# Cross-attention with a top-ten pick: the key-bias term moved to VectorE, and the second query projection placed behind the second weighted sum

## The reference

```python
scores = jnp.einsum('bnd,d->bn', base_hidden, score_w[0]) + score_b[0]
_, topk_idx = jax.lax.top_k(scores, TOPK)                       # TOPK = 10
sparse_hidden = jnp.take_along_axis(base_hidden, topk_idx[:, :, None], axis=1)
q = (sparse_hidden @ Wq.T + bq).reshape(B, TOPK, H, dh).transpose(0, 2, 1, 3)
k = (scaffold_hidden @ Wk.T + bk).reshape(B, -1, H, dh).transpose(0, 2, 1, 3)
v = (scaffold_hidden @ Wv.T + bv).reshape(B, -1, H, dh).transpose(0, 2, 1, 3)
logits = jnp.einsum('bhqd,bhkd->bhqk', q, k) * scale
attn = jax.nn.softmax(logits, axis=-1)
o = jnp.einsum('bhqk,bhkd->bhqd', attn, v).transpose(0, 2, 1, 3).reshape(B, TOPK, D)
attn_out = o @ out_w.T + out_b
return base_hidden.at[jnp.arange(B)[:, None], topk_idx].set(attn_out)
```

## Time and profile before

| | us |
|---|---|
| median of 3 runs | 140.95 (140.5 to 141.01) |
| the profiled execution | 140.47 |
| its span in the profile | 138.7 |
| TensorE busy | 132.0 (95%), 1314 instructions |
| VectorE busy | 91.7 (66%), 252 instructions |
| ScalarE busy | 27.0 (19%) |
| DMA over the span | 270 GB/s mean |

### The profile page before, as it was taken

How to read it: one execution, slowest core, us unless ns; L and a number is a source line. 1 busy time by engine, 2 the same in 40 slices (tenths; PEclk the granted TensorE clock), 3 DMA queues, 4 the chain that set the end, 5 groups by cost and what they waited for, 6 DMA issues and landing times.

```text
span 138.7 us, 3144 instructions
## 1 busy us (share of the span) xinstructions
PE 132.0 (95%) x1314; PEld 125.6 (91%) x1314; DVE 91.7 (66%) x252; ACT 27.0 (19%) x59; POOL 10.9 (8%) x36
## 2 busy tenths in 40 slices
PE   6889999999998999999999999999999999999990
PEld 3168999999997899999999999999999999999970
DVE  4596697898993676487872565177228799875160
ACT  5132400070511250012140041004101400131120
POOL 7710000260030000000000000000000000000002
PEclk9999999999999999999999999999999999999999
DMA  3999999999614999799999897998795093000001
GB/s 68 405 427 416 409 405 405 414 443 428 268 40 129 425 426 419 291 343 316 395 379 294 319 438 224 318 409 308 240 285 217 5 322 131 0 0 5 0 5 50
DMA packets 7293, 37.52 MB, mean 270 GB/s; under 512 B 1040, under 2 KB 1040, under 8 KB 5104
## 3 DMA queue, kind: packets, MB, share of 16 engines
q1 hardware_dynamic: 6864, 37.00, 70.6%
q0 software_dynamic: 128, 0.33, 0.8%
q10 hardware_dynamic: 288, 0.01, 0.1%
HBM read 33.50 MB, written 3.83 MB: 269 GB/s over the span
## 4 chain that ended last, share of the span: by engine, by line
PE 63%; DVE 14%; DMA 13%; SPq 4%; issue 4%; POOLq 1%; POOL 0%; DVEq 0%
PE mix_ps L899 29%; PE logits_ps L862 24%; DMA x_sb<-x_lines_dram 11%; PE logits_ps L846 5%; DVE product L442 3%; DMA picked<-x_dram,row_idx 2%; DVE col_max L569 2%; SPq L220 2%; PE logits_ps L818 2%; DVE probs L603 1%; PE mix_ps L818 1%; SPq L209 1%; DVE q_diag L530 1%; POOLq L62 1%; PE logits_ps L784 1%
## 5 line engine op out<-in xcount | busy, mean ns | idle before, releaser
L899 PE MATMUL mix_ps<-probs,ctx_r 125*128 125x160 f32 x336 | 47.2, 300 | 0.0
L899 PEld LDWEIGHTS mix_ps<-probs,ctx_r 125*128 125x128 f32 x336 | 46.0, 190 | 0.3 <-issue 0.2
L862 PE MATMUL logits_ps<-qk,ctx_c 128*125 128x160 f32 x240 | 33.4, 299 | 0.0
L862 PEld LDWEIGHTS logits_ps<-qk,ctx_c 128*125 128x125 f32 x240 | 32.9, 188 | 0.0
L569 DVE TENSOR_REDUCE col_max<-logits_ps 125x160 f32<-125x480 f32 x16 | 10.1, 653 | 16.6 <-PE logits_ps L862 13.7
L846 PE MATMUL logits_ps<-qk,ctx_c 128*125 128x160 f32 x144 | 20.1, 300 | 0.0
L846 PEld LDWEIGHTS logits_ps<-qk,ctx_c 128*125 128x125 f32 x144 | 19.6, 188 | 0.1
L388 ACT ACTIVATE mix<-mix_ps 128x320 f32<-128x320 f32 x16 | 7.0, 440 | 62.7 <-PE mix_ps L899 57.7
L610 DVE TENSOR_REDUCE prob_sum<-probs 125x160 f32<-125x960 f32 x8 | 14.6, 1829 | 4.5 <-ACT probs L378 4.4
L378 ACT ACTIVATE probs<-probs 125x480 f32<-125x480 f32 x16 | 9.3, 602 | 25.3 <-DVE probs L603 25.3
L442 DVE CUSTOM_DVE_ANT_0 product<-x_sb,score_w_sb 112x513 f32<-112x513 f32 x14 | 10.0, 761 | 2.4 <-DMA x_sb<-x_lines_dram 2.4
(11 more groups left out here) (137 smaller groups left out, 100.0 us busy)
## 6 DMA issues: line engine op xcount, KB each, us to landing
ctx_r<-ctx_rows_dram SPq DMA_DIRECT2D x7, 1536.0 KB, 10.2
ctx_c<-ctx_cols_dram SPq DMA_DIRECT2D x6, 1500.0 KB, 8.9
x_sb<-x_lines_dram SPq DMA_DIRECT2D x8, 520.0 KB, 13.0
out_dram<-x_sb SPq DMA_DIRECT2D x8, 448.0 KB, 9.7
ctx_r<-ctx_rows_dram SPq DMA_DIRECT2D x3, 512.0 KB, 15.5
ctx_c<-ctx_cols_dram SPq DMA_DIRECT2D x2, 750.0 KB, 14.4
ctx_c<-ctx_cols_dram SPq DMA_DIRECT2D x4, 375.0 KB, 15.1
wq_sb<-wq_dram SPq DMA_DIRECT2D x1, 1024.0 KB, 8.0
```

The costliest lines, as they stand in the source:

```text
L862: last = nc.tensor.matmul(logits_ps[n][0:S_P, t // BANK_T, (t % BANK_T) * HQ:(t % BANK_T + 1) * HQ], ctx_c[n][:, f, t, :], qk[:, b, f, :], ...
L899: last = nc.tensor.matmul(mix_ps[half][:, f * HQ:(f + 1) * HQ], ctx_r[n][0:S_P, t, c:c + P], probs[n][:, t, :], start=(t == 0), stop=(t == ...
```

## The change

The key-bias term no longer passes TensorE. `key_heads`, `dot_key_bias` and `spread_key_dot` go, and with them GpSimd's clearing of `key_heads`. VectorE multiplies the masked queries by the key bias, `key_terms` (one instruction for the first group, four for the second), and `sum_key_terms` adds over the partitions: a transposing reduction over 128 partitions, three copies, a small reduction.

The second group's masked queries are made by one instruction a block (`spread_pairs`): it reads the projection in PSUM, adds the bias and multiplies by the mask, into `q_pairs`, whose order is head, batch, query. The fold waits block by block for them.

On TensorE the transposes stand ahead of the 22nd matmul of the second weighted sum and the projection behind its last.

```diff
-        q_diag = [sb(f"q_diag{g}", [P, DT, b1 - b0, HPT, TOPK])
-                  for g, (b0, b1) in enumerate(GROUPS)]
+        q_diag = [sb("q_diag0", [P, DT, FIRST, HPT, TOPK])]
+        q_pairs = sb("q_pairs", [P, DT, HPT, GROUPS[1][1] - GROUPS[1][0], TOPK])
...
-        key_rows = sb("key_rows", [QUAD, B, DT, HC])
+        key_terms = sb("key_terms", [P, B, DT, HPT, TOPK])
...
+            def spread_pairs():
+                b0, b1 = GROUPS[1]
+                nb = b1 - b0
+                for e in range(DT):
+                    dve.wait_ge(q_ps, 3 + e // 2)
+                    nc.vector.scalar_tensor_tensor(
+                        out=q_pairs[:, e, :, :, :].rearrange("p h b q -> p h (b q)"),
+                        in0=query_ps[1][e // 2][:, (e % 2) * nb * TOPK:(e % 2 + 1) * nb * TOPK]
+                        .unsqueeze(1).broadcast_to([P, HPT, nb * TOPK]),
+                        scalar=bias_sb[:, 0, e:e + 1],
+                        in1=head_mask[:, :].unsqueeze(2).broadcast_to([P, HPT, nb * TOPK]), op0=ALU.add, op1=ALU.mult)\
+                        .then_inc(pair_q_done, 1)
...
+            def first_key_terms():
+                dve.wait_ge(q_done, 2)
+                nc.vector.tensor_tensor(
+                    key_terms[:, 0:FIRST, :, :, :].rearrange("p b e h q -> p e b (h q)"),
+                    q_diag[0][:, :, :, :, :].rearrange("p e b h q -> p e b (h q)"),
+                    bias_sb[:, 1, :].unsqueeze(2).unsqueeze(3).broadcast_to([P, DT, FIRST, HC]), ALU.mult).then_inc(key_terms_done, DT)
+
+            def pair_key_terms():
+                dve.wait_ge(pair_q_done, DT)
+                for e in range(DT):
+                    nc.vector.tensor_scalar(key_terms[:, FIRST:B, e, :, :].rearrange("p b h q -> p h b q"), q_pairs[:, e, :, :, :],
+                                            bias_sb[:, 1, e:e + 1], None, ALU.mult).then_inc(key_terms_done, 1)
+
+            def sum_key_terms(g):
...
+                dve.wait_ge(key_terms_done, DT * (g + 1))
                 nc.vector.tensor_reduce(
-                    key_dot[:, b0:b1, :].rearrange("p b k -> p (b k)"),
-                    key_rows[:, b0:b1, :, :].rearrange("p b e c -> p (b e c)").rearrange("p (k c) -> p k c", c=QUAD),
-                    AX.X, ALU.add, apply_transpose=True).then_inc(key_dot_done, 1)
+                    quad_sum[:, 0, bs, :].rearrange("p b k -> p (b k)"),
+                    key_terms[:, bs, :, :, :].rearrange("p b e h q -> p (b e h q)").rearrange("p (k c) -> p k c", c=QUAD),
+                    AX.X, ALU.add, apply_transpose=True).then_inc(key_step, 1)
+                dve.wait_ge(key_step, at + 1)
+                for q in range(1, QUADS):
+                    nc.vector.tensor_copy(quad_sum[0:QUAD, q, bs, :], quad_sum[q * QUAD:(q + 1) * QUAD, 0, bs, :]).then_inc(key_step, 1)
+                dve.wait_ge(key_step, at + 4)
+                nc.vector.tensor_reduce(key_dot[:, bs, :], quad_sum[0:QUAD, :, bs, :].rearrange("p q b k -> p b k q"), AX.X, ALU.add)\
+                    .then_inc(key_dot_done, 1)
...
             def fold_pairs():
                 w = HPT // 2 * TOPK * (GROUPS[1][1] - GROUPS[1][0])
-                pe.wait_ge(q_done, 4)
                 pe.wait_ge(shifted, 2 * GROUPS[0][1])
...
                     for e in range(DT):
+                        if step == 0:
+                            pe.wait_ge(pair_q_done, e + 1)
                         for r in range(2):
                             rows = slice(r * P // 2, (r + 1) * P // 2)
                             last = nc.tensor.matmul(pair_ps[step % 2][r][:, e * w:(e + 1) * w],
                                                     wk_sb[rows, e, step * P:(step + 1) * P],
-                                                    q_diag[1][rows, e, :, 2 * r:2 * r + 2, :],
+                                                    q_pairs[rows, e, 2 * r:2 * r + 2, :, :].rearrange("p h b q -> p b h q"),
                                                     start=True, stop=True)
...
-            weigh(1, 1, {18: transpose_picked, 21: lambda: project_queries(1)})
+            weigh(1, 1, {21: transpose_picked})
+            project_queries(1)
             fold_pairs()
-            dot_key_bias(1)
```

More of the change, by code:

```diff
@@ L518, in move_idx, with spread_queries @@
                     nc.vector.tensor_copy(row_idx[k * QUAD:k * QUAD + m, :], idx_cols[0:m, k:k + 1]).then_inc(idx_ready, 1)
[L520 to L522 removed]
+            def spread_queries():
                 for half in range(2):
                     es = slice(2 * half, 2 * half + 2)
[L525 removed]
+                    dve.wait_ge(q_ps, half + 1)
                     nc.vector.tensor_tensor(
[L527 to L529 removed]
+                        q_sb[:, es, :, :], query_ps[0][half][:, 0:2 * FIRST * TOPK].rearrange("p (t b q) -> p t b q", t=2, b=FIRST),
+                        bias_sb[:, 0, es].unsqueeze(2).unsqueeze(3).broadcast_to([P, 2, FIRST, TOPK]), ALU.add).then_inc(q_biased, 1)
+                    dve.wait_ge(q_biased, half + 1)
@@ L530, in spread_queries @@
                     nc.vector.tensor_tensor(
-                        q_diag[g][:, es, :, :, :].rearrange("p t b h q -> p (t b) h q"),
-                        q_sb[g][:, es, :, :].rearrange("p t b q -> p (t b) q").unsqueeze(2).broadcast_to([P, 2 * nb, HPT, TOPK]),
-                        head_mask[:, :].unsqueeze(1).unsqueeze(3).broadcast_to([P, 2 * nb, HPT, TOPK]), ALU.mult)\
+                        q_diag[0][:, es, :, :, :].rearrange("p t b h q -> p (t b) h q"),
+                        q_sb[:, es, :, :].rearrange("p t b q -> p (t b) q").unsqueeze(2).broadcast_to([P, 2 * FIRST, HPT, TOPK]),
@@ L701, in _ @@
             sum_probs(1, 1)
-            spread_queries(1)
+            spread_pairs()
             copy_pairs()
-            spread_key_dot(1)
+            pair_key_terms()
+            sum_key_terms(1)
             for b in range(2, B):
@@ L819, in fold_pairs @@
                                                     wk_sb[rows, e, step * P:(step + 1) * P],
-                                                    q_diag[1][rows, e, :, 2 * r:2 * r + 2, :],
+                                                    q_pairs[rows, e, 2 * r:2 * r + 2, :, :].rearrange("p h b q -> p b h q"),
                                                     start=True, stop=True)
                     last.then_inc(pair_done, 1)
-            def dot_key_bias(g):
-                w = TOPK * (GROUPS[g][1] - GROUPS[g][0])
-                pe.wait_ge(key_heads_done, 1)
-                pe.wait_ge(q_biased, 2 * g + 2)
-                for e in range(DT):
-                    last = nc.tensor.matmul(key_ps[g][e * QUAD:(e + 1) * QUAD, 0:w], key_heads[:, e, :],
-                                            q_sb[g][:, e, :, :].rearrange("p b q -> p (b q)"), start=True, stop=True)
-                last.then_inc(key_dot_ps, 1)
             def logits_by_step(b, n, copied, between):
```

37 lines of the change are left out of this document (10 added, 27 removed).

## The result

| us | before | changed |
|---|---|---|
| median, 8 runs each | 140.43 (140.16 to 141.01) | 139.17 (139.04 to 139.86) |
| ratio, 95% interval | | 0.991 (0.9892 to 0.9927) |
| profiled execution | 140.47 | 139.44 |
| span | 138.7 | 137.7 |

The change makes the kernel 0.9% faster.

What follows compares the result with a forecast made beforehand. TensorE was taken to bound the kernel, waiting only 0.76 us for the gather and 0.31 us for `q_diag`. Gains of 0.79 + 0.24 = 1.03 us, taken from 140.95, gave 139.9 us, range 139.4 to 140.8.

Steps and rivals of the forecast that it cites:

- What bounds the kernel: TensorE, with two gaps between 41 and 47 us; time won by 51.09 is kept to the end.
- Step 1: Second weighted sum on TensorE: three matmuls move into the 0.76 us gather wait, projection goes last; 0.82 us.
- Step 2: First key-bias product leaves TensorE, 0.18 us, worth nothing alone; VectorE's added work hides before `x_sb`, about 1.1 us spare.
- Step 3: One masked VectorE instruction a block, 0.46 us each; the fold's step 0 ends at 47.06 instead of 47.85: 0.79 us.
- The signs named, two waits of 0.1 to 0.2 us: TensorE waits inside step 0 of the fold, expected in the profile if the forecast is right.
- The instruction at half rate: VectorE's masked instruction might run at half throughput, near its upper bound of 0.66 us; gain 0.41 instead of 1.03 us.
- either fold rival: TensorE's fold reads its operand more slowly, gain 0.33 us, chance 0.06; or its row halves stop overlapping, 142.5, chance 0.05.
- Step 4: Second key-bias product leaves TensorE before batch 2's logits, 0.24 us; VectorE's replacement ends at 53.7 to 54.3, hidden.
- Step 5: Transfers: `load_rows(3, 1)`, queued behind batch 3's columns (6.6 us), lands at 49.1, needed at 56.8; costs nothing.
- The sum: Whole kernel: 0.79 + 0.24 = 1.03 us, subtracted from the shown median of 140.95 to give 139.9 us.
- low bound of step 3: Masked instructions of 0.28 us end the fold's step 0 at about 46.73: 0.33 us more gain, 139.6, chance 0.03.

Runs made afterwards that it cites:

- the third: The changed kernel with nothing altered, measured a third time beside the kernel before: 139.47 us, ratio 0.9934.
- block-wise projection's kernel: The changed kernel with the second projection finished block by block, each block with its own PSUM bank and signal: 138.67 us, ratio 0.9883 to before.
- key_only: The kernel before with only the key-bias term, both groups, moved to VectorE: 139.95 us, ratio 0.9965.
- second_only: The kernel before with only the second group's key-bias term moved to VectorE: 140.32 us, ratio 0.9992.
- late_scores: The changed kernel with six clearing instructions and their waits on VectorE ahead of the third batch's scores: 140.67 us, ratio 1.0 to the kernel before.

## Why the prediction was right in its mechanism and wrong in its time

- **What bounds the kernel**: right. What was won by 51.09 was kept to the end.
- **Step 1**, three matmuls in front of the gather: right in the first profile (42.42 in both). The spare time was too thin to be relied on: 0.26 us in that profile, 0.0 in the third.
- **Step 2**, the first key-bias product "worth nothing alone": mis-sized by 0.11 us. Its product of 320 elements took 0.49 us as taken, and the cover grew to 0.99 us (1.1 predicted), but the first maximum starts 0.11 us sooner after the scores. In two of the changed kernel's three profiles 0.06 and 0.09 of that were lost again ahead of batch 7's scores, whose `x_sb` landed just then.
- **Step 3**: right in its size, and partly lucky to 0.01 us. The new instruction took 0.47 us (0.46), four of them 1.78 us; the first fold step ended at 47.05 (47.06). But VectorE was sooner than forecast: the third instruction started at 45.83 (45.91), 0.12 us behind the projection and not 0.19, and the fourth was done at 46.68 (46.77). The fold gave that back: its last block began at 46.73 (46.81) and took 0.32 us, not four times 62 ns. The signs named, two waits of 0.1 to 0.2 us, are not quite what came; the blocks begin at 45.71, 46.03, 46.35 and 46.73. The instruction at half rate, against which the trace row spoke, didn't come. Nor did either fold rival: 12 runs of ten elements are read at the same 62 ns an instruction (0.99 us for 16 in the block-wise projection's kernel). The last two masked instructions and the last fold block:

```profile
45.83 0.84 DVE L535 SCALAR_TENSOR_TENSOR q_pairs<-logits_ps,bias_sb,head_mask 128x240 f32<-128x240 f32 x2
```

```profile
46.73 0.49 PE L836 MATMUL logits_ps<-q_pairs,wk_sb 64*128 64x120 f32 x4
```

- **Step 4**: right, 0.24 us in three kernels (the changed one, `key_only`, `second_only`); VectorE's second block ended at 54.02 (53.7 to 54.3).
- **Step 5**: right. The columns of batch 3 landed after 6.3 us, and nothing waited.
- **The step that failed is the last of "The sum"**: 1.03 us was subtracted from the median shown, 140.95. That median of three lay 0.5 us above what the kernel before takes (140.36 to 140.46 over five sets; the three were 140.5, 140.95, 141.01, and only the first is usual). From the profiled execution's own 140.47 the forecast would have been 139.44, just what the profiled execution of the changed kernel took, and within 0.3 us of the median. The exact match is luck: the start of batch 5's scores, on which the gather hangs, scatters from 21.29 to 21.94 us over the profiles without the six clearings. The prediction even said that the profiled execution stood 0.48 us below the median, and explained it by late transfers instead of asking whether three runs place a median. Of the 139.92 - 139.17 = 0.75 us, 140.95 - 140.43 = 0.52 is this, and 0.23 the gain (1.26 in this set against 1.03, 1.14 over three sets).
- **The range** had 0.5 us below the forecast: 0.33 from the low bound of step 3 and 0.2 for the median. The base alone was off by 0.52, so those 0.2 were the part that was too small; the three shown runs already spread over 0.5 us.

## What to carry to other kernels

A wait that is split by block can be worth more than the work it waits for: neither the new order (ratio 1.0007) nor the block-wise wait with the old order (0.9968, with the 0.24 us of the key-bias product in it) gave what they gave together, because work may leave a gap's place only when something else can fill it. When work is moved in front of an outside event, count how much earlier the engine arrives than the event in several executions, not in one. And a forecast in microseconds stands on two legs, the gain and the base: where the profiled execution and a median of three runs differ by half the gain, the base needs its own range.

## What the hardware showed that was not expected

- Beside GpSimd's product of two SBUF operands, one piece of VectorE's work is slow in every profile: a score of 0.69 us takes 1.75, or three small copies of 0.55 us together take 1.51 (`late_scores`). All of that is on the chain to the gather, some 1.0 us in every version. GpSimd's two instructions in the changed kernel, then in `late_scores`:

```profile
27.10 2.95 POOL L313 TENSOR_TENSOR mix<-x_sb,score_w_sb 112x513 f32<-112x513 f32 x2 [19.60 <-DMA x_sb<-x_lines_dram]
```

```profile
27.04 2.64 POOL L315 TENSOR_TENSOR mix<-x_sb,score_w_sb 112x513 f32<-112x513 f32 x2 [19.80 <-DMA x_sb<-x_lines_dram]
```

In `late_scores` each takes 1.28 us, the first ends at 28.32, and the slow copy runs from 27.22 to 28.34. In the changed kernel, where a score of VectorE starts at 28.22 ahead of GpSimd's second instruction, that one takes 1.60. So each engine seems to wait for the other's instruction to end. The Trainium skill says that the two share a pair of ports, which one of them holds for a whole instruction (SBUF — State Buffer, section Who interferes with whom); the traces agree, with these numbers. That GpSimd is the cause is read from the coincidence in time; moving that product was not tried.

- The start of the first maximum differs by 0.11 us with whether TensorE makes the first key-bias product, without any wait that the profile shows.
